# Moving the value tiles ahead of the row score tiles in TensorE's order of an attention stage

## The reference

```python
q, k, v = jnp.einsum('bsx,xAnh->Abnsh', input, w)
q = q + q_bias[:, None, :]
a = jnp.einsum('bnqh,bnkh->bnqk', q, k) * h ** (-0.5)
pos_scores = jnp.einsum('bnqh,nvh->bnqv', q, emb) * h ** (-0.5)
a = a + relative_causal(pos_scores)
a = jax.nn.softmax(jnp.where(mask, a, NEG_INF), axis=-1)
o = jnp.einsum('bnqk,bnkh->bqnh', a, v).reshape(b, s, n * h)
out = o @ (out_kernel * (fan_in * fan_out) ** (-0.25)) + out_bias
```

## Time and profile before

| | |
|---|---|
| median of 3 runs | 1332.55 us |
| profiled execution, its own time | 1332.87 us |
| its span, from first to last instruction | 1331.1 us |
| TensorE busy | 1192.1 us, 90% |
| VectorE, ScalarE, GpSimd busy | 829.3, 669.0, 827.9 us |
| first score tile of pairs 0 to 7, from the span's start | 487.1, 595.1, 700.9, 806.8, 912.6, 1018.4, 1124.2, 1230.0 us |

### The profile page before, as it was taken

How to read it: one execution, slowest core, us unless ns; L and a number is a source line. 1 busy time by engine, 2 the same in 40 slices (tenths; PEclk the granted TensorE clock), 3 DMA queues, 4 the chain that set the end, 5 groups by cost and what they waited for, 6 DMA issues and landing times.

```text
span 1331.1 us, 31072 instructions
## 1 busy us (share of the span) xinstructions
PE 1192.1 (90%) x11780; PEld 757.9 (57%) x11780; DVE 829.3 (62%) x2044; ACT 669.0 (50%) x1368; POOL 827.9 (62%) x1084
## 2 busy tenths in 40 slices
PE   4998599989936589999999999999999999999997
PEld 2354455657634225675566566566566566566665
DVE  3786447713565577667757756756866866765642
ACT  3443232246314226655665665665665655665664
POOL 1786100041302537888878878778788788787886
PEclk9998669999967659999999999999999999999998
DMA  8100100022111240112103103012023012121401
GB/s 327 74 0 1 40 1 1 1 71 78 26 63 52 51 107 18 41 40 51 41 18 73 41 18 73 20 39 65 10 42 77 14 41 60 31 42 23 115 2 33
DMA packets 75277, 64.02 MB, mean 48 GB/s; under 512 B 38996, under 2 KB 69208, under 8 KB 73560
## 3 DMA queue, kind: packets, MB, share of 16 engines
q1 hardware_dynamic: 74104, 59.94, 17.3%
q0 software_dynamic: 1024, 2.09, 0.5%
HBM read 21.52 MB, written 6.82 MB: 21 GB/s over the span
## 4 chain that ended last, share of the span: by engine, by line
PE 53%; ACT 4%; POOL 4%; DVE 3%; issue 3%; DMA 0%; DVEq 0%; POOLq 0%; ACTq 0%
PE S L1771 8%; PE A L1761 8%; PE S L1772 7%; PE S L1773 7%; PE O L1785 4%; PE O L1783 4%; PE O L1786 4%; ACT prob L1903 2%; PE M L1752 2%; POOL plow L1557 2%; PE M L1731 2%; PE M L1733 2%; PE M L1732 2%; DVE junk L1997 1%; PE M L1746 1%
## 5 line engine op out<-in xcount | busy, mean ns | idle before, releaser
L1557 POOL TENSOR_TENSOR plow<-prob 128x512 f16<-128x512 f32 (+3 forms) x640 | 590.8, 935 | 136.0 <-ACT prob L1903 112.5
L1903 ACT ACTIVATE prob<-S,keep_sigma 128x512 f32<-128x512 f32 (+3 forms) x640 | 387.0, 625 | 241.5 <-PE S L1773 240.2
L1997 DVE CUSTOM_DVE_ANT_0 junk<-A,mask_rows,part 128x512 bf16<-128x512 f32 (+3 forms) x384 | 248.6, 647 | 107.1 <-PE A L1761 77.2
L1783 PE MATMUL O<-V,prob 128*128 128x65 f16 x2176 | 233.7, 193 | 4.7 <-POOL plow L1557 4.7
L1771 PE MATMUL S<-rows 97*128 97x512 f16 (+3 forms) x640 | 224.5, 351 | 11.7 <-ACT prob L1903 11.3
L1785 PE MATMUL O<-V,prob 128*128 128x64 f16 x2176 | 233.3, 194 | 0.0
L1786 PE MATMUL O<-V,plow 128*128 128x65 f16 x2176 | 232.5, 192 | 0.0
L1772 PE MATMUL S<-rows 96*128 96x512 f16 (+3 forms) x640 | 223.6, 349 | 0.0
L1783 PEld LDWEIGHTS O<-V,prob 128*128 128x128 bf16 x2176 | 203.3, 97 | 30.5 <-POOL plow L1557 5.7
L1773 PE MATMUL S<-rows 96*128 96x512 f16 (+3 forms) x640 | 219.9, 347 | 0.0
L1761 PE MATMUL A<-rows 96*128 96x512 f16 (+3 forms) x640 | 206.8, 357 | 12.9 <-DVE negm L1997 7.0
(11 more groups left out here) (314 smaller groups left out, 1892.6 us busy)
## 6 DMA issues: line engine op xcount, KB each, us to landing
rows<-stage_rows SPq DMA_DIRECT2D x64, 256.0 KB, 3.5
V<-stage_v SPq DMA_DIRECT2D x16, 516.0 KB, 5.0
W<-in_W SPq DMA_DIRECT2D x2, 2048.0 KB
shifted<-turned SPq DMA_DIRECT2D x32, 128.0 KB, 2.3
rows<-stage_pos SPq DMA_DIRECT2D x64, 64.0 KB, 3.2
w<-in_w SPq DMA_DIRECT2D x2, 1024.0 KB
xe_rows<-zero SPq DMA_DIRECT2D x1, 1280.0 KB, 6.0
ye_rows<-xe SPq DMA_DIRECT2D x5, 256.0 KB, 3.1
```

The source lines that it names most:

```text
L1557: pool.tensor_tensor(plow[:, k % PB, 0:w], full, full.bitcast(BF16).rearrange("p (q e) -> p q e", e=2)[:, :, 1], ALU.subtract).then_inc(s_ ...
L1783: pe.matmul(both, high[:, cs, 1], vh[h][:, j, 0:HS + 1], start=(j == 0 and s == 0), stop=False, skip_group_check=True)
L1903: act.activation(prob[:, k % PB, 0:w], S[k % 2][:, 0:w], ACT.Exp, scale=sigma[:, 2 * p + h:2 * p + h + 1]).then_inc(s_exp, 1)
L1997: dve.tensor_tensor_reduce(junk[:, g % 2, 0:w], A[g % 2][:, 0:w], add, -1.0, before, ALU.add, ALU.min, out).then_inc(s_max, 1)
```

## The change

The diff exchanges two loops of TensorE's order. In each group the value tiles (of slots n-4 and n-3) now stand behind the score tiles and ahead of the row score tiles and items. No instruction is added, removed or altered, and no other engine's order changes.

```diff
@@ -1842,12 +1842,12 @@
                     if k < ALL:
                         score_tile(*divmod(k, SLOTS))
                 for k in two:
+                    if k >= DRAIN:
+                        value_tile(*divmod(k - DRAIN, SLOTS))
+                for k in two:
                     if k < ALL:
                         row_tile(*divmod(k, SLOTS))
                         slot_items(*divmod(k, SLOTS))
-                for k in two:
-                    if k >= DRAIN:
-                        value_tile(*divmod(k - DRAIN, SLOTS))
```

## The result

The change makes the kernel slower: 1388.45 us, median of four runs (1387.14 to 1391.9), against 1332.6 for the kernel before. The ratio is 1.0426, 95% interval 1.0403 to 1.0449. The profiled execution took 1387.14 us with a span of 1385.2. The forecast was 1382 us, range 1362 to 1398.

What follows compares the result with a forecast made beforehand. TensorE was taken as the bound, busy 90% of the span. Six middle pairs at 6.7 us (40.2), pair 0 6.3 and pair 7 2.2 add 48.7 to 1332.87: forecast 1382 us, range 1362 to 1398.

Steps and rivals of the forecast that it cites:

- What bounds it: In the seven pairs with all items, TensorE is the bound, with 2.9 us a pair of visible idle time to win.
- Step 1: Even-slot items ScalarE reads come up to 0.74 us later, delaying odd exponentials and later score tiles: 7.3 us a pair.
- Step 2: Row score tiles waiting for VectorE: waits at slots 51 and 45 gain 1.1 us a pair, slots 3 and 42 lose 0.4.
- The scaling: ScalarE's scaling at slots 46 and 70 waits a little longer for VectorE: 0.1 us a pair.
- The last pair: Pair 7: four turns cost 0.7 us each, less a 0.58 wait ahead of a maxima item: 2.2 us.
- Step 3: Pair start: row score tiles fall behind a value tile's wait for GpSimd; its 0.4 us is counted once, in Step 2.
- The price of the value pair: 24 value matmuls of 65 columns with weight loads take 0.74 us, 31 ns each, by the trace.
- A: Rival: faster, all visible TensorE waits in the pairs go and ScalarE's items cost nothing; 1311 us, chance 4%.
- B: Rival: no change, ScalarE's spare time hides the shift; 1333 us, chance 3%.
- C: Rival: much slower, late exponentials delay GpSimd and value tiles wait for it; 1440 us, mild form 1400, together 11%.
- D: Rival: slower by less, item delays overlap with existing score tile waits; 4 us a pair, 1363 us, chance 12%.
- E: Rival: TensorE's pauses of 0.7 to 1.4 us lower its clock to 1.2 GHz; chance 2%.

Runs made afterwards that it cites:

- the best order: Kernel before, with ScalarE's item copies and output scaling moved behind both exponentials of a group: ratio 0.9879 to the kernel before, pair 103.4 us.
- The undoing from TensorE's side: Changed kernel, with only the even slots' items moved ahead of the value tiles: ratio 1.0178 to the kernel before, pair 108.4 us.
- from ScalarE's side: Changed kernel, with ScalarE's item copies moved behind both exponentials of a group: ratio 1.0153 to the kernel before, pair 107.9 us.
- reciprocals-first run: Changed kernel, with VectorE's reciprocals moved ahead of the slot's row maximum: ratio 1.0413 to the kernel before, pair 112.8 us.
- with no waits for ScalarE: ScalarE's item copies and scaling moved behind both exponentials: ratio to the kernel before 0.9898 on the changed kernel, 0.9879 on the kernel before.

## Why the prediction was right

**What bounds it.** Right. The weight loads waiting for exponentials in the earlier trace rows pointed at the place. Only the 2.9 us of idle time "to be won" were too few a measure, as the drain of the matmul in front hides part of each wait: from start to start TensorE waited about 4.5 us a pair before (2.5 for exponentials, 1.3 for row maxima, 0.7 for GpSimd), and the best order takes 2.4 of them away.

**Step 1, the even items.** Right in mechanism, place and size for one group: 0.74 us lost at slots 18 and 19, by the rows above. For the pair it said 7.3, and the starts of the score tiles, before and after, bear this out place by place:

| score tiles of slots | behind items in slots | wait grows, forecast us | measured us |
|---|---|---|---|
| 19, 21, 23, 33, 51 | 16, 18, 20, 30, 48 | 0.74 each | 0.74, 0.73, 0.74, 0.74, 0.74 |
| 27, 29, 57 | 24, 26, 54 | 0.65, 0.28, 0.28 | 0.65, 0.28, 0.28 |
| 31, 45, 55, 75 | 28, 42, 52, 72 | little slack: 0.64 or more, 0.18 or more, 0.55 or more, 0.57 | 0.65, 0.24, 0.56, 0.56 |
| 11, 25, 63 | 8, 22, 60 | 0.12 each | 0.12, 0.13, 0.10 |
| together | | 7.3 | 7.2 |
| 49, 73 | scaling in 46, 70 | 0.1 together | 0.29, 0.23 |
| 53 | scaling in 50 | 0 | 0.43 |

No other score tile of the pair waits longer than before by more than 0.03 us. The undoing from TensorE's side gives 5.2 us and from ScalarE's side 5.7, with the late scaling under them. Fixing the reciprocals first and then moving the copies takes a pair from 112.8 to 104.1, 8.7 us, which includes what the kernel before was already losing there.

**Step 2, the row scores.** The absorbed wait came as foretold, and the sum is near. From start to start the row score tiles of slots 45 and 51 start 1.0 us less late, those of slots 2, 3 and 42 wait 0.5 more; 1.1 and 0.4 were forecast. TensorE in slots 50 and 51 of the kernel after, where the earlier trace rows answer: the two row score tiles stand together in one row, and the next score tile follows without a wait for VectorE.

```profile
898.60 0.36 PE L1761 MATMUL A<-rows 96*128 96x128 f16 x2
...
898.92 0.38 PE L1771 MATMUL S<-rows 97*128 97x512 f16 x1
...
900.00 0.39 PE L1771 MATMUL S<-rows 97*128 97x512 f16 x1 [0.27 <-ACT prob L1903]
```

**The scaling: the term that was mis-sized.** The last row shows it: a wait at slot 53, after a slot without a copy that could cause it (slot 50 has no item). I had 0.1 us a pair "for two places where the scaling on ScalarE waits a little longer for VectorE", slots 46 and 70, and 2.2 us for the last pair in all. ScalarE at slots 50 to 52 after:

```profile
898.75 0.93 ACT L1917 ACTIVATE otok<-O,rsum 128x64 f32<-128x64 f32 x4 [0.76 <-DVE rsum L2021]
899.56 0.38 ACT L1903 ACTIVATE prob<-S,keep_sigma 128x128 f32<-128x128 f32 x1
```

and VectorE:

```profile
897.88 0.74 DVE L1997 CUSTOM_DVE_ANT_0 junk<-A,mask_rows,part 128x512 bf16<-128x512 f32 x1
...
898.54 0.18 DVE L2021 RECIPROCAL rsum<-O 128x4 f32<-128x4 f32 x1
```

The reciprocal at 898.54 stands behind row maximum 49, the scaling starts at 898.75 after 0.76 us of idle time, exponential 51 follows at 899.56 and ends at 899.94, and score tile 53 starts 0.06 later. The prediction names slots 46 and 70 only. Slot 50, where the v item delays the row maximum in front of the reciprocal, was left out (0.43 us), and 46 and 70 were put too small (0.52 instead of 0.1). The reciprocals-first run puts the whole term at 0.8 us a pair, most of the 1.1 by which the pairs came out longer than forecast.

The last pair came out 3.1 us longer than forecast, and only 1.3 of that are waits of score tiles that go with the reciprocals first. The four turns cost 2.9, where 0.7 each was forecast. The wait ahead of a maxima item, which the value tiles were to fill with a gain of 0.58, did not go: this line is the same in both profiles of the last pair.

```profile
PE M L1742 <- DVE negm L1997: 0.4, 1, 0.4
```

And the row score tiles there, which the prediction did not count, wait 0.7 us more from start to start.

**Step 3, the start of a pair.** Right: the wait for GpSimd is 0.54 us before and after (the value tile of slot 1), with the row score tiles now behind it:

```profile
830.67 0.20 PE L1783 MATMUL O<-V,prob 128*128 128x65 f16 x1 [0.54 <-POOL plow L1557]
...
830.96 0.54 PE L1761 MATMUL A<-rows 96*128 96x512 f16 x2
```

**The price of the value pair.** 0.73 us in the profile after as well, 30 to 31 ns a matmul. The 81 ns that the prediction quotes from the Trainium skill ("TensorE: Matmul & The Clock Gate", section "Back-to-back issue gap") would by its estimate have given some 1490 us, so the measurement decides. It decides for 128 columns too: here are the last two matmuls of score tile 51, each with its own weight load, and the value matmul behind them.

```profile
897.75 0.22 PE L1772 MATMUL S<-rows 96*128 96x128 f16 x1
897.81 0.22 PE L1773 MATMUL S<-rows 96*128 96x128 f16 x1
897.86 0.19 PE L1783 MATMUL O<-V,prob 128*128 128x65 f16 x1
```

They are 0.05 to 0.06 us apart, and the median over all 588 matmuls with 128 columns of 16 bits in the attention is 55 ns.

**The rivals.** A and B fell with ScalarE's order; its 42 us of spare time did come into play, but only in the runs that change that order. C did not happen: GpSimd waits more for ScalarE (15.0 to 21.3 us), the value tiles' wait for it stayed at 0.5. D did not happen: less was merged than it supposes. E did not: the granted clock is 1.00 in the middle pair (2.4 GHz) with idle times of up to 1.3 us.

**The sum.** Pairs 1 to 6 gave 7.8 each instead of 6.7, pair 0 5.7 instead of 6.3, pair 7 5.3 instead of 2.2, together 57.7 instead of 48.7, 9 us too few. The untouched part ahead happened to be 3.6 us shorter in the profiled execution, which by luck brought the total nearer the forecast: with equal parts ahead it would have been 1390.7 us instead of 1387.1, still inside the range. For a middle pair the terms are, from start to start, 8.2 for the score tiles (7.2 and 0.9), less 0.5 for the row score tiles, and some 0.15 in differences below 0.03 us each.

## What to carry to other kernels

An engine with 40% of its time to spare can still be what another one waits for: look at what stands in front of the late instruction in that engine's own order, and when this is released. Whoever moves work on one engine should list every instruction of the others that follows it in order, not only its direct consumers; here one exchange of loops reached the exponentials by two ways, the item copies and the reciprocals. And when one repair gives less than it should, the profile of that run shows the second cause that lay under the first: alone the two repairs gave 5.7 and 0.8 us a pair, together 9.5.

## What was not expected of the hardware

Exchanging long and short matmuls costs TensorE next to nothing here: with no waits for ScalarE, a pair in the changed order takes 103.6 us and in the old one 103.4, and nearly all of that difference is a longer wait of row score tiles. The part ahead of the attention, the same code everywhere, took from 481 to 505 us in the profiled executions. Two things go with it. In its longest execution TensorE was granted the lower level, 1.2 GHz, for 154 us of that part, in its shortest for 126 (kernel before 143, change 133). And the four profiled executions on one chip took 481 to 488 us, the six on two other chips 496 to 505. What makes the clock and the chips differ stays open; the spread is more than most of the differences studied here, which is why the kernels were compared by pair.
